# Decay exponents by DMA broadcast in place of a matmul, and a new order of the output products

## The reference, cut to what matters

```
g = cumsum(g.reshape(Bb, H, N, chunk), axis=-1)
decay = where(lower, exp(g[..., :, None] - g[..., None, :]), 0)
A = where(strict, -(k_beta @ k.T) * decay, 0)
attn = solve_triangular(I - A, I)
v_c = attn @ (v * beta);  k_cumdecay = attn @ (k_beta * exp(g))
attn_i = where(lower, q_i @ k_i.T * d_i, 0)
o_i = q_i * exp(g_i) @ state + attn_i @ v_new
...
out = core * rsqrt(mean(core*core) + EPS) * norm_w * silu(z);  return out @ w_out
```

## Time and profile before

| what | value |
|---|---|
| three runs, median (lowest to highest) | 1486.92 us (1483.51 to 1491.84) |
| the profiled execution | 1484.96 us |
| its span, first to last instruction | 1483.2 us |
| PE busy | 1404.5 us, 95% of the span, 8400 matmuls |
| DVE busy | 1087.9 us, 73% |
| ACT busy | 845.7 us, 57% |
| POOL busy | 386.6 us, 26% |
| mean granted clock of PE | 0.991 |
| DMA | 63.41 MB, mean 43 GB/s |

### The profile page before, as it was taken

How to read it: one execution, slowest core, us unless ns; L and a number is a source line. 1 busy time by engine, 2 the same in 40 slices (tenths; PEclk the granted TensorE clock), 3 DMA queues, 4 the chain that set the end, 5 groups by cost and what they waited for, 6 DMA issues and landing times.

```text
span 1483.2 us, 23092 instructions
## 1 busy us (share of the span) xinstructions
PE 1404.5 (95%) x8400; PEld 802.8 (54%) x8400; DVE 1087.9 (73%) x2483; ACT 845.7 (57%) x1739; POOL 386.6 (26%) x319
## 2 busy tenths in 40 slices
PE   0879999999999999999999999998999999999998
PEld 0545755755665575475576567566444444444443
DVE  8898889889788888888978888875679775613000
ACT  4567667667677666766757766766443333212432
POOL 4311231050140132114015013115054443200332
PEclk9999999999999999999999999989999999999999
DMA  3000000010000000001001000002183445100220
GB/s 106 12 32 16 19 32 15 2 50 1 17 22 29 16 22 29 16 16 36 1 17 50 1 17 22 1 16 92 35 235 111 128 112 128 57 1 0 72 99 28
DMA packets 21512, 63.41 MB, mean 43 GB/s; under 512 B 4440, under 2 KB 7768, under 8 KB 20256
## 3 DMA queue, kind: packets, MB, share of 16 engines
q1 hardware_dynamic: 21120, 61.88, 13.5%
q10 hardware_dynamic: 288, 0.14, 0.1%
HBM read 59.61 MB, written 2.39 MB: 42 GB/s over the span
## 4 chain that ended last, share of the span: by engine, by line
PE 82%; DVE 10%; ACT 4%; DMA 1%; issue 1%; POOL 1%; DVEq 0%; ACTq 0%; SPq 0%; POOLq 0%
PE bank L488 13%; PE bank L1763 12%; PE bank L1741 11%; PE bank L525 7%; PE bank L566 6%; PE bank L1862 5%; PE bank L603 4%; PE bank L618 3%; DVE conv L1067 3%; PE bank L535 3%; PE bank L517 3%; PE bank L598 2%; ACT z L883 2%; PE bank L609 2%; PE bank L620 2%; PE bank L510 2%
## 5 line engine op out<-in xcount | busy, mean ns | idle before, releaser
L1067 DVE SCALAR_TENSOR_TENSOR conv<-bank,taps,conv 128x510 f32<-128x510 f32 (+2 forms) x384 | 283.9, 743 | 27.6 <-ACT conv L814 17.9
L488 PE MATMUL bank<-rT,wf 128*128 128x512 f32 x512 | 254.1, 611 | 2.8 <-DVE rT L250 1.9
L1613 POOL TENSOR_TENSOR ffn_weighted<-ffn_relu,ffn_wide 128x512 f32<-128x512 f32 x96 | 128.9, 1375 | 301.9 <-DMA ffn_wide<-ffn_shares 150.1
L1763 PE MATMUL bank<-ffn_weighted,feat 128*128 128x512 f32 x400 | 187.3, 597 | 4.2 <-POOL ffn_weighted L1613 4.2
L1741 PE MATMUL bank<-rT,feat 128*128 128x512 f32 x400 | 188.5, 598 | 0.0
L1624 ACT ACTIVATE ffn_relu<-bank 128x512 f32<-128x512 f32 x100 | 59.6, 596 | 179.7 <-PE bank L1741 179.7
L1301 POOL TENSOR_TENSOR sq<-sq,qsq 128x512 f32<-128x512 f32 x64 | 82.8, 1295 | 278.7 <-ACT sq L993 276.8
L488 PEld LDWEIGHTS bank<-rT,wf 128*128 128x128 f32 x512 | 89.7, 191 | 82.3 <-issue 72.2
L1763 PEld LDWEIGHTS bank<-ffn_weighted,feat 128*128 128x128 f32 x400 | 76.3, 191 | 100.7 <-issue 99.3
L1741 PEld LDWEIGHTS bank<-rT,feat 128*128 128x128 f32 x400 | 76.3, 192 | 93.8 <-issue 93.3
L525 PE MATMUL bank<-zs,wo 128*128 128x512 f32 x256 | 120.8, 603 | 0.0
(11 more groups left out here) (252 smaller groups left out, 2720.4 us busy)
## 6 DMA issues: line engine op xcount, KB each, us to landing
ffn_wide<-ffn_shares SPq DMA_DIRECT2D x64, 256.0 KB, 5.3
feat<-in_L_chunks_dram SPq DMA_DIRECT2D x25, 512.0 KB, 3.6
wf<-in_wf_dram SPq DMA_DIRECT2D x8, 1024.0 KB, 4.8
wz<-in_wz_dram SPq DMA_DIRECT2D x8, 512.0 KB, 3.3
wo<-in_wo_dram SPq DMA_DIRECT2D x8, 512.0 KB, 3.4
ffn_wide<-ffn_shares SPq DMA_DIRECT2D x8, 512.0 KB, 4.4
m<-in_fT_dram SPq DMA_DIRECT2D x2, 512.0 KB, 4.8
xT<-in_xT_dram SPq DMA_DIRECT2D x1, 1024.0 KB, 8.8
```

Source lines behind the costliest of these rows:

```text
L488: ins = pe.matmul(banks[bank_of(p, n)][:], wf[:, c, ORDER[n // NH], :], rT[:, c, halves(n % NH)], start=(c == 0), stop=(c == CT - 1))
L1067: dve.scalar_tensor_tensor(acc[:, :, k:], src[:, :, 0:T - k], taps[:, ORDER[n // NH], KS - 1 - k:KS - k], acc[:, :, k:], ALU.mult, ALU.add ...
L1613: pool.tensor_tensor(hw[:, j, u, :], h2[:, j, u, :], wide[:, j, u // NH % BLOCKS, halves(u % NH)], ALU.mult).then_inc(weighted, 1)
L1763: last = pe.matmul(banks[4 + 2 * c + h][:], chunk[:, slot, CT + t, c * P:(c + 1) * P], of, start=start, stop=stop, skip_group_check=True)
```

## The change

1. The sums' rows stay f32 (32 rows instead of three times 32). SP writes them to DRAM, `decay_rows`, laid out per value head and stretch as 256 + 128 columns, and loads them back for each step, spread to all 128 partitions (`load_decay`), into five buffers laid over `z`: five steps at once (`load_first`), the other three as buffers come free. `sel`, `identb`, `eye3`, the bf16 `rows` and the PE function `decay` go.
2. POOL adds the mask in place (`hide`), two steps ahead at the end of the previous group, six at the group's start. ACT's exponential works in place.
3. PE's step loop holds one output product between gram 0 and gram 1, two between later grams and one behind the last.
4. In the first group six v units get their last tap from ACT (`own_and_last`, into `zs`) and POOL (`add_tap`), two instead of three from DVE (`convolve_two`).
5. Two small loads move ahead of the first feature weights on SP, and some semaphores are merged.

The queue now waits for the rows' sums and for the store behind `slice`, and five loads stand ahead of `wz`. The core of the diff:

```diff
+    def store_rows(sp):
+        by_tile = grow.rearrange("h (s r t) -> h s r t", s=B, r=2)
+        sp.wait_ge(sums_read, ROWS_READ)
+        sp.dma_start(room["rows_dram"][:, :, 0:2, :], by_tile).then_inc(rows_out, 16)
+        sp.dma_start(room["rows_dram"][:, :, 2, :], by_tile[:, :, 1, :]).then_inc(rows_out, 16)
+        sp.wait_ge(rows_out, 32)
...
+        def load_decay(g, n):
+            v, s = g * GV + 2 * (n // B), n % B
+            sp.dma_start(dec[n % ND], rows_dram[v:v + 2, s, :, :].rearrange("v r t -> v (r t)").partition_broadcast(P))\
+              .then_inc(dec_in[n % ND], 16)
+        def load_first(g):
+            for n in range(ND):
+                if g:
+                    sp.wait_ge(mix_full, (g - 1) * NU + NH * (((n + 1) * 6 * P - 1) // NT) + NH)
+                load_decay(g, n)
...
+            for n in range(ND, GK * B):
+                sp.wait_ge(m_ready, g * PAIRS + 2 * (n - ND) + 2)
+                load_decay(g, n)
...
             gram(g, 0)
-            pe.wait_ge(sel_ready, g + 1)
...
-            decay(g, 0)
             if not first:
+                pe.wait_ge(og_ready, before - 1)
+                output(g - 1, 0, 4, 0)
                 pe.wait_ge(conv_ready, (g + 1) * NF * NH)
             gram(g, 1)
-            decay(g, 1)
             for n in range(1, GK * B):
                 if n >= 2:
                     pe.wait_ge(m_ready, g * PAIRS + 2 * n - 2)
                     gram(g, n)
-                    decay(g, n)
                 if not first:
...
-                    output(g - 1, (n - 1) // 4, 4 + (n - 1) // 4, (n - 1) % 4)
+                    for k in (2 * n - 1, 2 * n):
+                        output(g - 1, k // GV, 4 + k // GV, k % GV)
...
+        def own_and_last(n):
+            act.activation(conv[:, n % HF, :], banks[bank_of(0, n)][:], ACT.Copy, scale=taps[:, ORDER[n // NH], KS - 1:KS])
+            act.activation(by_seq(last_tap(n), 2)[:, :, KS - 1:], by_seq(banks[bank_of(0, n)][:], 2)[:, :, 0:T - KS + 1],
+                           ACT.Copy, scale=taps[:, ORDER[n // NH], 0:1]).then_inc(conv0_ready, 1)
...
-                act.wait_ge(decay_full, g * PAIRS + i + 1)
-                act.activation(dec[i % 4][:, 0:T], banks[6 + r][:, 0:T], ACT.Exp, bias=gcol[:, v, 2 * s:2 * s + 1])
+                if r == 0:
+                    act.wait_ge(masked, g * GK * B + n + 1)
+                act.activation(e[:, 0:T], e[:, 0:T], ACT.Exp, bias=gcol[:, v, 2 * s:2 * s + 1])
...
-            dve.tensor_copy(sel[:], eye3[:, hs].unsqueeze(2).to_broadcast([96, GV, P])).then_inc(sel_ready, 1)
...
+        def add_tap(n):
+            pool.wait_ge(tapped, 2 * (n + 1))
+            acc = by_seq(conv[:, n % HF, :], 2)
+            pool.tensor_tensor(acc[:, :, KS - 1:], acc[:, :, KS - 1:], by_seq(last_tap(n), 2)[:, :, KS - 1:],
+                               ALU.add).then_inc(conv_ready, 1)
+        def hide(g, n):
+            pool.wait_ge(dec_in[n % ND], 16 * uses(g, n))
+            ends = dec[n % ND].rearrange("p r (a t) -> p r a t", a=3)[:, :, 0::2, :]
+            pool.tensor_tensor(ends, ends, mask[:].unsqueeze(1).unsqueeze(1).to_broadcast([P, 2, 2, P]),
+                               ALU.add).then_inc(masked, 1)
```

More of the change, by code:

```diff
@@ L335 @@
 KQ = HD * HD * 1e-6
+SHARED_TAPS = HF + 2
+AHEAD = 2
+ND = 5
 EVICTS = 20
@@ L352, in delta_phase @@
     EPS, EPSQ = cols[:, 0:1], cols[:, 1:2]
-    beta, neg_g, rows, eye3, mask, identb, wu, tout, fac = (
-        keep[k] for k in ("beta", "neg_g", "rows", "eye3", "mask", "identb", "wu", "tout", "fac"))
+    beta, neg_g, mask, wu, tout, fac = (keep[k] for k in ("beta", "neg_g", "mask", "wu", "tout", "fac"))
     ident = env["ident"]
@@ L461, in group @@
                 load_slice(g)
-            if not last:
+            if not first:
+                load_first(g)
+            if not first and not last:
                 sp.wait_ge(conv0_ready, (g + 1) * NF * NH)
                 load_features(sp, g + 1)
+            for n in range(ND, GK * B):
+                sp.wait_ge(m_ready, g * PAIRS + 2 * (n - ND) + 2)
+                load_decay(g, n)
+            if first:
+                sp.wait_ge(conv0_ready, NF * NH)
+                load_features(sp, 1)
             sp.wait_ge(tr_ready, g * TURNS + 2)
@@ L470, in sync @@
         load_slice(0)
+        front["store_rows"](sp)
+        load_first(0)
         groups(sp, group)
@@ L537, in gram @@
                       start=True, stop=True).then_inc(gram_full, 1)
-        def decay(g, n):
-            kh, s = n // B, n % B
-            t0, t1 = s * T, s * T + P
-            for r in range(2):
-                i = 2 * n + r
-                if i >= 2:
-                    pe.wait_ge(dec_ready, g * PAIRS + i - 1)
-                e = banks[6 + r]
-                pe.matmul(e[:, 0:T], sel[:, 2 * kh + r, :], rows[:, t0:t0 + T], start=True, stop=False,
-                          skip_group_check=True)
-                pe.matmul(e[:, T:T + P], sel[:, 2 * kh + r, :], rows[:, t1:t1 + P], start=False, stop=False,
-                          skip_group_check=True)
-                pe.matmul(e[:, 0:P], identb[:], mask[:], start=False, stop=False, skip_group_check=True)
-                pe.matmul(e[:, T:T + P], identb[:], mask[:], start=False, stop=True,
-                          skip_group_check=True).then_inc(decay_full, 1)
         def turn_v(g, n):
@@ L695, in filler @@
                         pe.wait_ge(conv_ready, p * NF * NH + n - 3)
-                    elif first:
-                        pe.wait_ge(dec_ready, PAIRS)
-                    else:
+                    elif not first:
                         pe.wait_ge(out_added, g * 4 + n - 3)
@@ L1069, in convolve, with convolve_two @@
                                              tapped if k < KS - 1 else conv_ready, 1)
+        def convolve_two(n):
+            acc, src = by_seq(conv[:, n % HF, :], 2), by_seq(banks[bank_of(0, n)][:], 2)
+            dve.wait_ge(conv0_ready, n + 1)
+            for k in (1, 2):
+                if k > 1:
+                    dve.wait_ge(tapped, 2 * n + k - 1)
+                dve.scalar_tensor_tensor(acc[:, :, k:], src[:, :, 0:T - k], taps[:, ORDER[n // NH], KS - 1 - k:KS - k],
+                                         acc[:, :, k:], ALU.mult, ALU.add).then_inc(tapped, 1)
         def add_output(g, u, b):
@@ L1317, in group @@
             if first:
-                pool.wait_ge(sel_ready, 1)
+                pool.wait_ge(heads_done, 1)
+                pool.wait_ge(front["rows_out"], 32)
                 pool.memset(pT[:], 0.0).then_inc(zeroed, 1)
+                pool.wait_ge(front["heads_in"], 80)
+                for n in range(AHEAD):
+                    hide(0, n)
+            for n in range(AHEAD, GK * B):
+                hide(g, n)
+                if first:
+                    add_tap(HF + n)
             pool.wait_ge(tr_ready, g * TURNS + 1)
@@ L1335, in group @@
                     multiply(g, n - 2)
+                if n >= NU - AHEAD and g < NG - 1:
+                    hide(g + 1, n + AHEAD - NU)
             for n in (NU - 2, NU - 1):
```

167 lines of the change are left out of this document (74 added, 93 removed).

## The result

The changed kernel took 1480.07 us (median of 20 runs, 1469.04 to 1486.37), the kernel before 1486.3 (20 runs, 1483.25 to 1491.84). The ratio is 0.9949, 95% interval 0.9934 to 0.9963 (the medians alone give 0.9958): a gain of half a per cent, of just the size that can be told from none. The profiled execution took 1477.17 us with a span of 1475.4, against 1484.96 and 1483.2. The 20 times spread over 17 us where those of before spread over 9.

What follows compares the result with a forecast made beforehand. PE was taken as the bound, DVE's inverse 2.2 us behind. Gains of 6.7 + 1.8 - 0.1 = 8.4 us off 1484.96 gave 1476.6, plus 1.96 to the median: 1478.5, range 1470 to 1487; faster below 1479.5.

Steps and rivals of the forecast that it cites:

- DVE's inverse is the second bound, and takes over: End of a group: DVE's inverse is 2.2 us behind PE and becomes late next; gain 1.9 us a group, not 4.4.
- A step of 3.06, the last `m` 0.1 late: Groups 1 to 6, step loop: gram plus two output products take 3.06 us; last `m` counted 0.1 late.
- PE idle 2.6 ahead of gate 5: Before the second four gates: PE, done early with outputs, waits 2.6 us in the timeline for ACT's first SiLU.
- The clock: 1.6 us in 6 of 10 groups: Gates 5 to 8: after the idle stretch PE's clock may halve, losing 1.6 us; taken as 6 in 10.
- Six groups, 6.7 us: Groups 1 to 6: 1.1 us a group after weighing clock falls, 6.7 us in all.
- Group 0, 1.8 us: First group, DVE-bound: fewer convolution taps less added delays gain 1.8 us; last `m` near 105.2 instead of 107.0.
- Group 7, 0.1 lost: Last group, without projections: PE already waited 2.24 us for the inverse, so no gain and 0.1 us lost.
- From the profile to the median: Whole run: 1.96 us added to the forecast profiled execution, 1476.6, to give the forecast median, 1478.5.
- Masks of 2.54 a step would still be hidden: Step loop, later groups: POOL's mask addition, taken as 1.27 us, would stay under PE's 3.06 even at 2.54.
- a clock that never falls: Rival, groups 1 to 6: full clock behind the idle stretch, 1.9 us gained each, 1473.7 us; chance 0.21.
- one that always falls: Rival, groups 1 to 6: clock falls in every group, 0.6 us gained each, 1481.6 us; chance 0.20.
- The slower one: Rival, step loops: DVE's `m` and POOL block each other, 0.96 us per POOL operation, 1497 us; chance 0.08.

## Why the prediction was right, and where it was off

- *DVE's inverse is the second bound, and takes over.* Right. `below32` started 26.9 (at most 27.3) behind the last `m` wherever the clock stayed up and PE was not itself the later one; filling or shortening PE's wait ahead of gate 5 didn't move it.
- *A step of 3.06, the last `m` 0.1 late.* 0.05 a step too long, and 0.22 in the first: gram 2 came 3.11 behind gram 1, not 3.33, the other steps were 3.01, and the last `m` came 0.33 earlier after gram 1 than before. Without a fall a group gained 2.3 us instead of 1.9.
- *PE idle 2.6 ahead of gate 5.* 2.70.
- *The clock: 1.6 us in 6 of 10 groups.* It fell in 5 of 7 groups in the first profile, 6 of 7 in the second, 5 of 7 with the masks doubled and 2 of 7 with the taps undone: 18 of 28. The price was 1.6 for most and 3.0 for the longer one of group 4, which I had not allowed for.
- *Six groups, 6.7 us.* Last `m` of group 1 to last `m` of group 7 took 731.25 before and 725.76 after: 5.5, and 0.25 more from group 0's last `m` to group 1's.
- *Group 0, 1.8 us.* The step that was mis-sized. Its `below32` came 0.6 earlier. The first `m` was 0.65 late, as forecast, and the convolutions saved their 4.6; but first to last `m` became 29.4, not 28.2. I had called POOL's tap, mask and exponential "just hidden" by DVE's 3.63. In the trace DVE waited 1.49 for an exponential that stood behind POOL's tap and mask, and 0.67 for ACT's last tap; with masks first first to last `m` takes 27.0 and both waits are gone.
- *Group 7, 0.1 lost.* Nothing gained behind its last `m`, as said.
- *The rest.* 0.6 + 5.7 = 6.3 us came from the loop against 8.4 forecast. Behind the start of group 7's `below32` the profiled execution took 1.5 us less, by luck: that stretch follows the clock, as the table shows. With it the sum is 7.8.
- *From the profile to the median.* I added 1.96 us; it was 2.9. The median came out 1.6 above the 1478.5 forecast and 0.6 above the line of 1479.5, under which I had put 0.52 of the chances; the ratio's interval leaves out 1 all the same.
- *A broadcast of 384 KB lands in 4 to 8.* 3.9. POOL waited 13 us in all for the loads, nothing else did.
- *Masks of 2.54 a step would still be hidden.* Wrong: 3.2 us a group. The argument compared POOL's rate with PE's and left out that POOL starts late, that two of the additions stand ahead of work that the next group waits for, and that DVE's operations on the slice then run beside POOL. It was no term of the sum.

Of the rivals, a clock that never falls (1473.7) and one that always falls (1481.6) are both cases of the same kernel: its 20 times lie from 1469 to 1486, and neither of its two profiles had seven falls of seven or none. The slower one, POOL and DVE's `m` blocking each other, fell with `m` at 743 ns (744 before).

What the forecast did not see is how the parts share the result. The decays by DMA alone bring 1.05% (0.77 to 1.33); with the shared taps it is 1.43% (1.19 to 1.67), but the trace gives the sharing 1.2 us, 0.08%; of the rest, the profiles have 2.6 us in groups 1 and 2 and 2.6 behind the loop, and the two intervals overlap, so the sharing has no share of its own that the times show. The two products between grams then take most of it back, to 0.51%. In the profiles that last step costs 14.3 us up to group 7's `below32`: 8.2 for falls and the like, 0.6 for each of six periods, and 2.4 for the later last `m` in group 7. The sum came out near since I worked out the whole.

## What to carry over

When two engines meet at one point, move work so that both arrive together: here one product a step fits beside DVE, two more fill PE's waits there, and the seven behind the last gram cover ACT. With more of them between, PE delays the inverse and then waits for ACT. Ask of each wait you create whether the clock may fall behind it and what runs then: large matmuls lost 1.6 us, the small ones of an inverse 12.

## What the runs showed of the hardware

A wait of the same length, 2.70 us at the same place, was followed by a fall of the clock in 18 of 28 cases, and in different groups in two executions of one kernel; waits of 2.0 to 2.4 ahead of the inverse's small matmuls were followed by one in 2 of 6. Filling the wait with matmuls whose result nobody reads took all falls away, 0 of 7, and made the loop 5.5 us shorter; one period was still 1.8 us longer than the usual one.
